# Attention value matmuls placed one unit later, with two tiles for the transposed probabilities, in a cross-attention and expert layer

## The chip, the cores and the metric

The kernel runs on one core of one Trainium2 chip. The metric is the device time of one execution in microseconds. The median of three executions of the kernel before is 782.37 us (781.3 to 784.15).

## The reference, cut to what matters

```
x = x + xattn(layernorm(x), ctx, ctx, pad, sub, Wq, bq, Wk, bk, Wv, bv)
x = x + ffn(layernorm(x), Ws1, bs1, Ws2, bs2, We1, be1, We2, be2, Wr, br)

xattn:  q, k, v = query @ Wq.T + bq, key @ Wk.T + bk, value @ Wv.T + bv     # 16 heads of 16
        att = where(pad or sub is 0, -1e9, q k^T / sqrt(16))
        out = softmax(att) v
ffn:    ys = geglu(x @ Ws1 + bs1) @ Ws2 + bs2                               # shared expert
        logits = (x @ Wr + br) / 1.5 ; top 2 of 12 experts, softmax over the two
        yr = sum over the two of weight * (geglu(x @ We1[e] + be1[e]) @ We2[e] + be2[e])
        return ys + yr
```

x and ctx are (16, 128, 256) in f32: 16 batches of 128 rows. The change is in the attention and in what stands directly before and behind it.

## The kernel before, in words

**Pairs and units.** Attention runs over eight pairs of batches (`pair(p, ...)`, once in the code of each engine). A pair has four units, n = 0 to 3: unit n covers batch n // 2 of the pair and the eight heads of half n % 2. Pair 0 stands alone (`first`), pairs 1 to 4 are a hardware loop of two pairs a turn, pairs 5 and 6 are written out, and so is pair 7 (`last`), which has no projections to make for a next pair.

**What a unit does.** TensorE makes the scores of eight heads in two banks of `ps_s` (`scores`: two mask matmuls, L476, and sixteen small ones, L481). VectorE takes the negated maximum (L1011) and adds it while it copies the scores to SBUF (`softmax_shift`, L1017, tile `prob`); ScalarE takes the exponential in place (`exp`, L775). In the next unit TensorE transposes the probabilities in two halves of four heads (`prob_transposes`, jj = 0 and 1, L493), both into the same bank `ps_t[:, 0]`, and ScalarE copies each half to `probT` (`prob_copy`, L766). The second half can be transposed only when the first has been copied. `values` (L505) then multiplies all eight heads of `probT` by v into `ps_o`. When both halves of a batch are in `ps_o`, ScalarE copies it to `outT` (`out_copy`, L771), TensorE transposes it back (`out_transposes`, L514), and VectorE divides by the row sums (`norm`, L1025 and L1027), adds to x and takes statistics (`residual`, L1035 to L1043). With both batches of a pair added, GpSimd raises the variance to -1/2 (`rstd`, L1286 and L1288) and VectorE writes the second layer norm (`ln2_apply`, L1051).

**The steps of the next pair.** Between a unit's transposes and values stand the steps that prepare pair p + 1: `cT` and `xT` (transposes of context and of normalised x), `k0`, `k1`, `q0`, `q1` (two projections of k and two of q) and `v`; and two for pair p - 1: `r` (transposes of the second layer norm) and `l` (router logits). The table `PLAN` says which steps stand in which unit. Every step takes the next of two PSUM banks (`step_bank`). For `cT` and `xT` ScalarE copies a high part to `aTh` (L743) and VectorE takes the rest to `aTl` (L948); for a k step the two are `k_hi` (L754) and `k_lo` (L958), for a q step `q_cut` (L751) and `q_st` (L955). A step on TensorE waits until the step two before it has left its bank (semaphore `xb_free`), and a pair's first scores wait for every step of the pair before.

**What sets the order.** Each engine runs its own instructions in the order in which its block lists them, and `pair` lists them by hand for each engine: TensorE at L533, ScalarE at L798, VectorE at L1055. An engine that waits holds up everything listed behind. On VectorE, unit 0's `cT` step stands between maximum and shift; `norm(p, 0)` is in unit 2, `norm(p - 1, 1)` in unit 0, and the residuals one unit behind each.

**Before and behind.** Ahead of pair 0 the same seven steps are made once for pair 0 (`PROJ`), with the weights split into high and low parts just ahead of their first use: `weights_hi` on ScalarE (L737), `weights_lo` on VectorE (L940). VectorE makes the masks at the `v` step (L985 to L993); at the `k1` step it waits for the rest of x (semaphore `x_rest_in`) and makes the first layer norm of pair 1 (L903 to L913). SyncE issues the loads. Behind pair 7 the feed-forward part begins (`up`, L583) while the last batch is finished. GpSimd then scatters rows to the experts, and the expert tiles follow. None of these is edited.

Of the kernel before, what the change touches and what calls it, by code (L numbers as in the profile page):

```python
# [17 lines left out]
P = 128  # L18
# [30 lines left out]
def build(nc, x_d, ctx_d, pad_d, sub_d, wq_d, wk_d, wv_d, bq_d, bk_d, bias_d, tab_d, ws1_d, ws2_d, w1_d,  # L49
# [98 lines left out]
    probT = put("probT", [P, 2, 4, P], f32, low)  # L148
# [121 lines left out]
    PLAN = [["cT", "xT", "k0"], ["v", "k1"], ["r", "q0"], ["q1", "l"]]  # L270
# [37 lines left out]
    with block:  # L308
# [3 lines left out]
        def _(sp):  # L312
# [3 lines left out]
            sp.dma_start(wk_raw[:, :, :], wk_d.rearrange("(c p) n -> p c n", p=P)).then_inc(wk_in, 16)  # L316
            sp.dma_start(wv_raw[:, :, :], wv_d.rearrange("(c p) n -> p c n", p=P)).then_inc(wv_in, 16)
            sp.dma_start(wq_raw[:, :, :], wq_d.rearrange("(c p) n -> p c n", p=P)).then_inc(wq_in, 16)
# [93 lines left out]
        def _(pe):  # L412
# [42 lines left out]
            def router(s, q, idx, bank):  # L455

                pe.wait_ge(xb_free, idx - (0 if isinstance(idx, int) and idx == PAIR_STEPS_END + 1 else 1))
# [38 lines left out]
            def values(U, n, par, batch):  # L496
# [4 lines left out]
                for g in range(4):  # L501
                    for jj in range(2):
# [3 lines left out]
                                          probT[:, jj, g, :], start=True, stop=True)  # L506
# [11 lines left out]
            for k, s in enumerate(PROJ):  # L518
                if s == "xT":
                    pe.wait_ge(idents_ready, 1)  # L520
                if s == "k0":
                    pe.wait_ge(w_ready, 1)
                if s == "v":
                    pe.wait_ge(w_ready, 2)
                    pe.wait_ge(bias_ready, 1)
                if s == "q0":
                    pe.wait_ge(w_ready, 3)
                step(s, 0, 0, k, k % 2)
# [4 lines left out]
            def pair(p, par, first, last):  # L533
                for n in range(4):
# [6 lines left out]
                    pn, ppar, pbatch = (n - 1) % 4, par if n else 1 - par, p * 2 + (n - 1) // 2  # L541
# [10 lines left out]
                    if prev:  # L552
                        prob_transposes(p * 4 + n - 1, pn, 0)
                    next_step()
                    if prev:
                        prob_transposes(p * 4 + n - 1, pn, 1)
                    next_step()
                    if prev:
                        values(p * 4 + n - 1, pn, ppar, pbatch)
                    next_step()  # L560
                    if n % 2 == 0 and prev:
# [112 lines left out]
            x_transposes(0, 0, 0)  # L674
            prob_transposes(UNITS - 1, 3, 1)
            values(UNITS - 1, 3, 1, B - 1)
            pe.wait_ge(converted, 1)
            pe.wait_ge(shifted, UNITS)
            up(0, 0, 0, False, SH)
            out_transposes(B - 1)  # L680
            up(0, 0, 1, False, SH)
# [43 lines left out]
        def _(sc):  # L725
# [13 lines left out]
            def step(s, pp, par, idx, bank):  # L739
# [16 lines left out]
                else:  # L756
                    sc.wait_ge(xb_free, idx)
                    act.activation(v_sb[par][:, :, :, 0:HD],
# [3 lines left out]
            def prob_copy(U, jj):  # L762
                sc.wait_ge(pt_ready, 2 * U + jj + 1)
                if not (isinstance(U, int) and U == 0):
                    sc.wait_ge(pv_done, 2 * U + jj - 1)
                act.activation(probT[:, jj, :, :], ps_t[:, 0, :].rearrange("p (g t) -> p g t", g=4),  # L766
# [19 lines left out]
            for k, s in enumerate(PROJ):  # L786
                if k == 1:
                    weights_hi(wkh, wk_raw, wk_in)
                if s == "v":
                    weights_hi(wvh, wv_raw, wv_in)  # L790
                    weights_hi(wqh, wq_raw, wq_in)
# [6 lines left out]
            def pair(p, par, first, last):  # L798
                for n in range(4):
# [13 lines left out]
                    if prev:  # L813
                        prob_copy(U, 0)
                    next_step()
                    if prev:
                        prob_copy(U, 1)
                    if n == 0:
                        next_step()
                    if n % 2 == 0 and prev:  # L820
                        out_copy(p * 2 + (n - 1) // 2)
                    exp(p * 4 + n, n)
# [42 lines left out]
            prob_copy(UNITS - 1, 0)  # L865
            x_hi(0)
            prob_copy(UNITS - 1, 1)
# [22 lines left out]
        def _(ve):  # L890
# [79 lines left out]
            for k, s in enumerate(PROJ):  # L970
# [4 lines left out]
                if s == "v":  # L975
                    weights_lo(wvl, wv_raw, wvh, 1)
                    weights_lo(wql, wq_raw, wqh, 2)
# [77 lines left out]
            def pair(p, par, first, last):  # L1055
                for n in range(4):
# [12 lines left out]
                    if n == 3:  # L1069
# [396 lines left out]
```

## Time and profile before

| | |
|---|---|
| median of three executions | 782.37 us |
| the profiled execution | 781.65 us, span 779.5 us |
| TensorE matmul busy | 640.2 us (82%) |
| VectorE busy | 457.8 us (59%) |
| ScalarE busy | 270.1 us (35%) |
| GpSimd busy | 330.0 us (42%) |
| before the first scores | 0 to 30.3 us |
| attention, pairs 0 to 7 | 30.3 to 256.4 us |
| routing, scatter and expert tiles | 256.4 to 779.5 us |

Busy shares over the whole span mix stages with different limits, so the attention is read pair by pair. In the rows below a time is in microseconds from the span's start. A timeline row gives the start, the duration, the engine, the line, the operation, and what is written from what; where the engine sat idle before it, the idle time and what ended it stand in brackets. SPq is the queue of SyncE. PEclk is the granted TensorE clock as a share of 2.4 GHz, so 0.50 is 1.2 GHz.

### The profile page before, as it was taken

What the parts mean: (1) busy time and instruction counts of PE and PEld (TensorE: products, weight loads), DVE (VectorE), ACT (ScalarE), POOL (GpSimd) and SP (SyncE); (2) the same over time, 40 slices, a digit from 0 to 9 for tenths busy, and PEclk for the clock granted to TensorE, in tenths of its full rate; (3) what the DMA queues carried; (4) which work ended last, traced back from release to release, by engine and by line L of the source; (5) the groups of instructions that cost most, each with busy time, mean ns of one, the idle gap of its engine ahead of it and who ended that gap; (6) DMA issues with size and microseconds to landing.
All of it is one profiled execution on the core that took longest, in us unless ns stands there. A gap on an engine that the chain in (4) does not pass through costs nothing.

```text
span 779.5 us, 16006 instructions
## 1 busy us (share of the span) xinstructions
PE 640.2 (82%) x4977; PEld 590.3 (76%) x4978; DVE 457.8 (59%) x893; ACT 270.1 (35%) x556; POOL 330.0 (42%) x389
## 2 busy tenths in 40 slices
PE   4699899899987776079999999999999999997041
PEld 4577777777865665079999999999999999997041
DVE  4656677676765583056665656656566565663136
ACT  3245555555544311024333333333333333331010
POOL 0610000000000477790847957677878582006710
PEclk9689999999999898579999999999999999999556
DMA  9930101001001143252344435525554241013412
GB/s 305 371 133 15 42 28 40 13 27 42 1 29 41 42 148 109 101 189 61 104 162 150 161 119 191 161 76 193 189 177 153 101 135 40 27 40 99 118 48 81
DMA packets 44289, 83.03 MB, mean 107 GB/s; under 512 B 4832, under 2 KB 32736, under 8 KB 44128
## 3 DMA queue, kind: packets, MB, share of 16 engines
q0 software_dynamic: 11120, 48.24, 18.4%
q1 hardware_dynamic: 32560, 34.04, 13.2%
q10 hardware_dynamic: 576, 0.30, 0.2%
q8 instruction: 21, 0.34, 0.2%
q14 instruction: 12, 0.10, 0.0%
HBM read 60.81 MB, written 19.66 MB: 103 GB/s over the span
## 4 chain that ended last, share of the span: by engine, by line
PE 71%; DVE 8%; another core or an unknown queue 8%; issue 5%; ACT 5%; SPq 1%; DMA 1%; POOL 0%; DVEq 0%; ACTq 0%
PE ps_s L583 27%; PE ps_o L623 15%; PE ps_t L596 5%; PE ps_t L493 4%; PE ps_s L481 4%; PE ps_o L505 4%; PE ps_t L440 3%; ACT probT L766 2%; PE ps_x L440 2%; PE ps_s L476 2%; DVE x_all L1264 2%; PE ps_x L605 1%; DMA br<-in_br 1%; DVE ag L1176 1%
## 5 line engine op out<-in xcount | busy, mean ns | idle before, releaser
L583 PE MATMUL ps_s<-ring,xTh 128*128 (+1 forms) x944 | 203.0, 337 | 4.9 <-issue 4.4
L623 PE MATMUL ps_o<-ring,hTh 128*128 (+1 forms) x644 | 127.3, 297 | 65.6 <-DVE hTl L1188 59.0
L583 PEld LDWEIGHTS ps_s<-ring,xTh 128*128 128x128 f32 x944 | 155.3, 193 | 8.3 <-issue 5.4
L623 PEld LDWEIGHTS ps_o<-ring,hTh 128*128 128x128 f32 x644 | 103.1, 198 | 67.4 <-issue 57.3
L1298 POOL TENSOR_TENSOR ring<-stage,ring 128x512 fp32r<-128x512 f32 x120 | 150.9, 1287 | 2.3
L1176 DVE TENSOR_TENSOR ag<-ps_s,up_bias 128x768 f32<-128x768 f32 (+1 forms) x96 | 88.8, 925 | 67.0 <-PE ps_s L583 45.4
L838 ACT ACTIVATE hTh<-ps_t 128x384 fp32r<-128x384 f32 (+1 forms) x118 | 54.6, 462 | 207.1 <-PE ps_t L596 138.9
L583 PE MATMUL ps_s<-ring,xTl 128*128 (+1 forms) x472 | 115.5, 325 | 2.1 <-issue 2.0
L1286 POOL TENSOR_TENSOR ve<-mv,eps 128x2 f32<-128x2 f32 x16 | 3.1, 197 | 232.4 <-DVE mv L1043 170.9
L623 PE MATMUL ps_o<-ring,hTl 128*128 (+1 forms) x322 | 93.3, 290 | 0.0
L831 ACT ACTIVATE ps_s<-ag 128x384 f32<-128x384 f32 (+1 forms) x118 | 55.1, 467 | 90.7 <-DVE ag L1176 85.4
L583 PEld LDWEIGHTS ps_s<-ring,xTl 128*128 128x128 f32 x472 | 83.8, 192 | 0.6 <-issue 0.6
L1182 DVE TENSOR_TENSOR ag<-ag,ps_s 128x384 f32<-128x384 f32 (+1 forms) x118 | 61.1, 518 | 37.6 <-ACT ps_s L831 31.1
L1188 DVE TENSOR_TENSOR hTl<-ps_t,hTh 128x384 fp32r<-128x384 f32 (+1 forms) x118 | 60.9, 517 | 23.6 <-ACT hTh L838 19.1
L1294 POOL TENSOR_SCALAR ring<-stage 128x512 fp32r<-128x512 f32 x120 | 71.7, 626 | 4.8 <-DVE logits L966 4.0
L596 PE MATMUL ps_t<-const,ag 128*128 128x128 f32 x322 | 57.1, 282 | 8.3 <-issue 7.5
L623 PEld LDWEIGHTS ps_o<-ring,hTl 128*128 128x128 f32 x322 | 63.8, 198 | 0.0
L766 ACT ACTIVATE probT<-ps_t 128x512 f32<-128x512 f32 x64 | 38.2, 596 | 69.5 <-PE ps_t L493 69.5
L1409 POOL DMA_INDIRECT gath<-rows_out,idx_top x32 | 30.8, 961 | 67.1 <-DMA rows_out<-y_row 57.6
L1193 DVE TENSOR_TENSOR xTl<-ps_x,xTh 128x256 fp32r<-128x256 f32 x59 | 25.0, 424 | 50.9 <-ACT xTh L845 44.5
L596 PEld LDWEIGHTS ps_t<-const,ag 128*128 128x128 f32 x322 | 38.5, 143 | 15.0 <-issue 10.4
L1011 DVE TENSOR_REDUCE nmax<-ps_s 128x8 f32<-128x1024 f32 x32 | 39.0, 1220 | 16.6 <-PE ps_s L481 16.5
(194 smaller groups left out, 1018.6 us busy)
## 6 DMA issues: line engine op xcount, KB each, us to landing
stage<-in_w POOLq DMA_DIRECT2D x12, 1536.0 KB, 6.7
stage<-in_w POOLq DMA_DIRECT2D x12, 768.0 KB, 5.4
up_bias<-in_bias POOLq DMA_DIRECT2D x12, 768.0 KB, 4.8
rows_in<-y_row SPq DMA_DIRECT2D x1, 5504.0 KB, 22.3
xrow<-rows_in SPq DMA_DIRECT2D x43, 128.0 KB
rows_out<-y_row SPq DMA_DIRECT2D x43, 128.0 KB, 1.7
cbuf<-in_ctx SPq DMA_DIRECT2D x8, 256.0 KB, 3.2
xn_all<-xn2p SPq DMA_DIRECT2D x8, 256.0 KB, 2.4
```

The costliest lines, as they stand in the source:

```text
L583: last = pe_.matmul(out, x[:, c, :], weights(place, a, half_w), start=n == 0, stop=n == 5)
L596: last = pe_.transpose(ps_t[:, u, c * P:(c + 1) * P], ag[u][:, 0, c * P:(c + 1) * P], ident)
L623: pe_.matmul(ps_o[:, 0:D], h[u][:, c, :], weights(place, a, D), start=n == 0, stop=False)
L766: act.activation(probT[:, jj, :, :], ps_t[:, 0, :].rearrange("p (g t) -> p g t", g=4), ACT.Identity).then_inc(pt_copied, 1)
L831: act.activation(ps_s[:, 2 * u + 1, 0:half_w], ag[u][:, 1, 0:half_w], ACT.Gelu).then_inc(gelu_done[u], 1)
L838: act.activation(hTh[u][:, 0:nch, :], ps_t[:, u, 0:nch * P].rearrange("p (c n) -> p c n", c=nch), ACT.Identity).then_inc(ht_hi[u], 1)
L1011: vec.tensor_reduce(nmax[:, :, :], src, AX.X, ALU.max, negate=True).then_inc(maxed, 1)
L1176: vec.tensor_tensor(ag[u][:, :, 0:half_w], ps_s[:, 2 * u:2 * u + 2, 0:half_w], bias, ALU.add)\
L1182: vec.tensor_tensor(ag[u][:, 0, 0:half_w], ag[u][:, 0, 0:half_w], ps_s[:, 2 * u + 1, 0:half_w], ALU.mult)\
L1188: vec.tensor_tensor(hTl[u][:, 0:nch, :], ps_t[:, u, 0:nch * P].rearrange("p (c n) -> p c n", c=nch), hTh[u][:, 0:nch, :].bitcast(f32), ALU ...
L1294: last = pool.tensor_scalar(hi_ap[:, c:c + PIECE], src[:, c:c + PIECE], 1.0, 0.0, ALU.mult, ALU.add)
L1298: last = pool.tensor_tensor(lo_ap[:, c:c + PIECE], src[:, c:c + PIECE], hi_ap[:, c:c + PIECE].bitcast(f32), ALU.subtract)
```

## The change

`probT` becomes two tiles, taken by turns of the unit. On TensorE `values` of unit n - 2 stands between the two halves of the transposes of unit n - 1, and `out_transposes` stands at the end of units 1 and 3 in place of 0 and 2. `PLAN` moves `q0` to unit 1, `v` alone to unit 2, and `r`, `q1`, `l` to unit 3. ScalarE takes the exponential and the `out_copy` ahead of the second `prob_copy`. VectorE has `norm`, `residual` and `ln2_apply` one unit later. Ahead of pair 0 the v weights come after the q weights, in the loads as well.

```diff
@@ -145,7 +145,10 @@
 ...
     prob = [put(f"prob{i}", [P, 2, 4, P], f32, low) for i in range(2)]
-    probT = put("probT", [P, 2, 4, P], f32, low)
+    probT = [put("probT0", [P, 2, 4, P], f32, low)]
+    spare = [ring_at + 2 * SLOT_W * 4 + 2 * (W1S + W2S) * 4]
+    probT.append(put("probT1", [P, 2, 4, P], f32, spare))
+    assert spare[0] <= ring_at + 3 * SLOT_W * 4
     assert low[0] <= ring_at + 2 * SLOT_W * 4, low[0] - ring_at - 2 * SLOT_W * 4
@@ -267,7 +270,7 @@
-    PLAN = [["cT", "xT", "k0"], ["v", "k1"], ["r", "q0"], ["q1", "l"]]
+    PLAN = [["cT", "xT", "k0"], ["k1", "q0"], ["v"], ["r", "q1", "l"]]
     PROJ = [s for unit in PLAN for s in unit if s not in "rl"]
@@ -314,8 +317,8 @@
 ...
             sp.dma_start(wk_raw[:, :, :], wk_d.rearrange("(c p) n -> p c n", p=P)).then_inc(wk_in, 16)
+            sp.dma_start(wq_raw[:, :, :], wq_d.rearrange("(c p) n -> p c n", p=P)).then_inc(wq_in, 16)
             sp.dma_start(wv_raw[:, :, :], wv_d.rearrange("(c p) n -> p c n", p=P)).then_inc(wv_in, 16)
-            sp.dma_start(wq_raw[:, :, :], wq_d.rearrange("(c p) n -> p c n", p=P)).then_inc(wq_in, 16)
             sp.dma_start(sub_b[:, :], sub_d).then_inc(mask_in, 16)
@@ -454,7 +457,7 @@
 ...
-                pe.wait_ge(xb_free, idx - (0 if isinstance(idx, int) and idx == PAIR_STEPS_END + 1 else 1))
+                pe.wait_ge(xb_free, idx - (0 if isinstance(idx, int) and idx in (PAIR_STEPS_END - 1, PAIR_STEPS_END + 1) else 1))
                 ps = step_bank[bank]
@@ -503,7 +506,7 @@
 ...
                         last = pe_.matmul(ps_o[32 * j:32 * j + VW, g * P:(g + 1) * P], v_sb[par][:, b, h, :],
-                                          probT[:, jj, g, :], start=True, stop=True)
+                                          probT[n % 2][:, jj, g, :], start=True, stop=True)
                         if g == 3:
@@ -520,11 +523,11 @@
 ...
                     pe.wait_ge(w_ready, 1)
+                if s == "q0":
+                    pe.wait_ge(w_ready, 2)
                 if s == "v":
-                    pe.wait_ge(w_ready, 2)
+                    pe.wait_ge(w_ready, 3)
                     pe.wait_ge(bias_ready, 1)
-                if s == "q0":
-                    pe.wait_ge(w_ready, 3)
                 step(s, 0, 0, k, k % 2)
@@ -538,7 +541,8 @@
 ...
                     prev = not (first and n == 0)
-                    pn, ppar, pbatch = (n - 1) % 4, par if n else 1 - par, p * 2 + (n - 1) // 2
+                    behind = not (first and n < 2)
+                    pn, ppar, pbatch = (n - 2) % 4, par if n >= 2 else 1 - par, p * 2 + (n - 2) // 2
@@ -550,15 +554,15 @@
 ...
                     if prev:
-                        prob_transposes(p * 4 + n - 1, pn, 0)
+                        prob_transposes(p * 4 + n - 1, (n - 1) % 4, 0)
                     next_step()
+                    if behind:
+                        values(p * 4 + n - 2, pn, ppar, pbatch)
                     if prev:
-                        prob_transposes(p * 4 + n - 1, pn, 1)
+                        prob_transposes(p * 4 + n - 1, (n - 1) % 4, 1)
                     next_step()
-                    if prev:
-                        values(p * 4 + n - 1, pn, ppar, pbatch)
                     next_step()
-                    if n % 2 == 0 and prev:
+                    if n % 2 == 1 and behind:
                         out_transposes(pbatch)
@@ -672,13 +676,14 @@
 ...
             x_transposes(0, 0, 0)
+            values(UNITS - 2, 2, 1, B - 1)
             prob_transposes(UNITS - 1, 3, 1)
-            values(UNITS - 1, 3, 1, B - 1)
             pe.wait_ge(converted, 1)
 ...
             up(0, 0, 0, False, SH)
+            values(UNITS - 1, 3, 1, B - 1)
+            up(0, 0, 1, False, SH)
             out_transposes(B - 1)
-            up(0, 0, 1, False, SH)
             router("r", PAIRS - 1, PAIR_STEPS_END, 0)
@@ -755,15 +760,17 @@
 ...
                     sc.wait_ge(xb_free, idx)
+                    if not (isinstance(pp, int) and pp < 2):
+                        sc.wait_ge(pv_done, pp * 8 - 8)
                     act.activation(v_sb[par][:, :, :, 0:HD],
 ...
-            def prob_copy(U, jj):
+            def prob_copy(U, n, jj):
                 sc.wait_ge(pt_ready, 2 * U + jj + 1)
-                if not (isinstance(U, int) and U == 0):
-                    sc.wait_ge(pv_done, 2 * U + jj - 1)
-                act.activation(probT[:, jj, :, :], ps_t[:, 0, :].rearrange("p (g t) -> p g t", g=4),
+                if not (isinstance(U, int) and U < 2):
+                    sc.wait_ge(pv_done, 2 * U - 2)
+                act.activation(probT[n % 2][:, jj, :, :], ps_t[:, 0, :].rearrange("p (g t) -> p g t", g=4),
                                ACT.Identity).then_inc(pt_copied, 1)
@@ -786,9 +793,10 @@
 ...
                     weights_hi(wkh, wk_raw, wk_in)
+                if s == "q0":
+                    weights_hi(wqh, wq_raw, wq_in)
                 if s == "v":
                     weights_hi(wvh, wv_raw, wv_in)
-                    weights_hi(wqh, wq_raw, wq_in)
                 if s == "k0":
@@ -811,15 +819,13 @@
 ...
                     if prev:
-                        prob_copy(U, 0)
+                        prob_copy(U, (n - 1) % 4, 0)
                     next_step()
+                    exp(p * 4 + n, n)
+                    if n % 2 == 1 and not (first and n < 2):
+                        out_copy(p * 2 + (n - 2) // 2)
                     if prev:
-                        prob_copy(U, 1)
-                    if n == 0:
-                        next_step()
-                    if n % 2 == 0 and prev:
-                        out_copy(p * 2 + (n - 1) // 2)
-                    exp(p * 4 + n, n)
+                        prob_copy(U, (n - 1) % 4, 1)
                     next_step()
@@ -862,9 +868,9 @@
 ...
-            prob_copy(UNITS - 1, 0)
+            prob_copy(UNITS - 1, 3, 0)
             x_hi(0)
-            prob_copy(UNITS - 1, 1)
+            prob_copy(UNITS - 1, 3, 1)
             out_copy(B - 1)
@@ -973,8 +979,9 @@
 ...
                 if s == "v":
-                    weights_lo(wvl, wv_raw, wvh, 1)
-                    weights_lo(wql, wq_raw, wqh, 2)
+                    weights_lo(wvl, wv_raw, wvh, 2)
+                if s == "q0":
+                    weights_lo(wql, wq_raw, wqh, 1)
                     vec.tensor_scalar(bqc[:, :], bqs[:, :], const[:, C_LOQ:C_LOQ + 1], None, ALU.mult)\
@@ -1066,20 +1073,20 @@
 ...
                     softmax_shift(p * 4 + n, n, next_step if n == 0 and todo else None)
-                    if n == 3:
-                        residual(p, 0)
-                    if n == 1 and not first:
+                    further = not last and not (isinstance(p, int) and p + 2 >= PAIRS)
+                    if n == 0 and not first:
+                        residual(p - 1, 0)
+                    if n == 2 and not first:
                         residual(p - 1, 1)
-                    further = not last and not (isinstance(p, int) and p + 2 >= PAIRS)
-                    if n == 1 and not first:
-                        ln2_apply(p - 1)
                     if n == 2 and further:
                         ln1_stats(p + 2)
-                    if n == 2:
-                        norm(p, 0)
                     while todo:
                         next_step()
-                    if n == 0 and not first:
+                    if n == 2 and not first:
+                        ln2_apply(p - 1)
+                    if n == 3:
+                        norm(p, 0)
+                    if n == 1 and not first:
                         norm(p - 1, 1)
@@ -1220,6 +1227,7 @@
 ...
+            residual(PAIRS - 1, 0)
             x_lo(0)
```

**TensorE, unit 0 of a pair in the loop, behind its scores.** `ps_t` and `ps_x` are PSUM banks, the number behind `prob` and `probT` tells the tile. Before:

```order
L493 MATMUL ps_t<-const,prob_119 128x128 x4
L425 REGISTER_ALU
L431 ISA
L417 MATMUL ps_x<-const,cbuf 128x128 x4
L491 REGISTER_ALU
L493 MATMUL ps_t<-const,prob_119 128x128 x4
L417 MATMUL ps_t<-const,xn_121 128x128 x4
L498 REGISTER_ALU
L505 MATMUL ps_o<-probT,v_sb_116 32x128 x8
```

Of the change:

```order
L496 MATMUL ps_t<-const,prob_119 128x128 x4
L428 REGISTER_ALU
L434 ISA
L420 MATMUL ps_x<-const,cbuf 128x128 x4
L501 ISA
L503 REGISTER_ALU
L508 MATMUL ps_o<-probT_120,v_sb_116 32x128 x8
L494 REGISTER_ALU
L496 MATMUL ps_t<-const,prob_119 128x128 x4
L420 MATMUL ps_t<-const,xn_122 128x128 x4
```

The values now read the other `probT` and stand between the two halves, where before they came behind both.

**ScalarE, unit 3 of a pair in the loop.** Before, the whole unit:

```order
L766 ACTIVATE probT<-ps_t 128x512
L741 REGISTER_ALU
L751 ACTIVATE q_cut<-ps_t,bqc,const 128x256 x2
L763 ISA
L766 ACTIVATE probT<-ps_t 128x512
L774 REGISTER_ALU
L775 ACTIVATE prob_119<-prob_119 128x1024
```

Of the change, from the router's copy to the unit's end:

```order
L790 ACTIVATE xn2T<-ps_x 128x512
L781 REGISTER_ALU
L782 ACTIVATE prob_119<-prob_119 128x1024
L777 ISA
L778 ACTIVATE outT<-ps_o 128x512
L770 REGISTER_ALU
L773 ACTIVATE probT_120<-ps_t 128x512
L746 REGISTER_ALU
L756 ACTIVATE q_cut<-ps_t,bqc,const 128x256 x2
```

The last q projection's `q_cut` was ahead of the unit's exponential; it is now behind the exponential and two copies.

**VectorE, ahead of pair 0, from the k1 step on.** `wql` and `wvl` are the low parts of the q and v weights, `xn` the first layer norm of pair 1. Of the change:

```order
L964 SCALAR_TENSOR_TENSOR k_lo_114<-ps_t,bks,k_hi_112 128x256 x2
L1004 MEMSET v_sb_116 128x32x15
L1005 MEMSET v_sb_116 128x32
L1004 MEMSET v_sb_117 128x32x15
L1005 MEMSET v_sb_117 128x32
L909 BN_STATS bn_67<-x_all 128x6 x2
L911 MEMSET tick 128x1
L913 BN_AGGR mv_68<-bn_67 128x2 x2
L919 TENSOR_SCALAR xn_122<-x_all,mv_68,rs_70 128x256 x2
L946 TENSOR_TENSOR wql<-wq_raw,wqh 128x1024
L985 TENSOR_SCALAR bqc<-bqs,const 128x4
L961 SCALAR_TENSOR_TENSOR q_st_110<-ps_x,bqs,q_cut 128x256 x2
```

Before, `wvl` and `wql` stood ahead of the masks, of the k1 step's `k_lo` and of the wait for the rest of x; now `wql` stands behind that wait, and `wvl` behind the first `q_st`.

## Rows read from the trace of the kernel before

**Rows 1.** Stretches of pairs 0, 3 and 7: PE, PEld, DVE, ACT, POOL busy us (instructions), PEclk, DMA.

```profile
30.30:62.30 32.00, 28.51 (x218) 23.44 (x218) 17.34 (x30) 13.14 (x22) 10.86 (x12) 0.75 0.52 183
...
118.10:145.98 27.88, 25.58 (x259) 21.58 (x259) 19.42 (x43) 15.09 (x26) 1.77 (x4) 1.00 0.09 28
...
228.80:256.40 27.60, 20.27 (x215) 15.05 (x215) 14.10 (x25) 11.79 (x18) 0.88 (x2) 1.00 0.10 30
```

**Rows 2.** Timeline of TensorE in pair 3.

```profile
138.87 0.66 PE L514 MATMUL ps_o<-const,outT 128*128 128x128 f32 x4 [0.72 <-ACT outT L771]
```

**Rows 3.** Timeline of ScalarE in pair 3.

```profile
129.81 0.59 ACT L766 ACTIVATE probT<-ps_t 128x512 f32<-128x512 f32 x1
130.29 1.05 ACT L775 ACTIVATE prob<-prob 128x1024 f32<-128x1024 f32 x1
131.24 0.84 ACT L754 ACTIVATE k_hi<-ps_x,bks 128x256 fp32r<-128x256 f32 x2
...
139.66 1.01 ACT L751 ACTIVATE q_cut<-ps_x,bqc,const 128x256 fp32r<-128x256 f32 x2
```

**Rows 4.** Timeline of VectorE in pair 3.

```profile
122.16 1.22 DVE L1017 TENSOR_TENSOR prob<-ps_s,nmax 128x1024 f32<-128x1024 f32 x1
...
126.04 0.88 DVE L958 SCALAR_TENSOR_TENSOR k_lo<-ps_x,bks,k_hi 128x256 fp32r<-128x256 f32 x2 [2.06 <-ACT k_hi L754]
126.83 0.25 DVE L1025 RECIPROCAL rden<-ps_o 128x16 f32<-128x16 f32 x1
...
127.46 1.22 DVE L1011 TENSOR_REDUCE nmax<-ps_s 128x8 f32<-128x1024 f32 x1
128.80 1.23 DVE L1017 TENSOR_TENSOR prob<-ps_s,nmax 128x1024 f32<-128x1024 f32 x1
129.94 0.41 DVE L1035 TENSOR_TENSOR x_all<-x_all,att 128x256 f32 x1
...
132.39 0.74 DVE L1051 TENSOR_SCALAR xn2p<-x_all,mv,rs 128x256 f32 x2 [1.29 <-POOL rs L1288]
133.04 0.87 DVE L958 SCALAR_TENSOR_TENSOR k_lo<-ps_x,bks,k_hi 128x256 fp32r<-128x256 f32 x2
...
144.78 0.86 DVE L955 SCALAR_TENSOR_TENSOR q_st<-ps_t,bqs,q_cut 128x256 fp32r<-128x256 f32 x2
145.55 0.17 DVE L966 TENSOR_TENSOR logits<-ps_x,br 128x24 f32 x1
```

**Rows 5.** Timeline of SyncE's queue at the start.

```profile
4.35 0.45 SPq L321 DMA_DIRECT2D x_all<-in_x  x1
```

**Rows 6.** DMA issues at the start: tile, queue, count, KB, us from issue to landing.

```profile
x_all<-in_x SPq DMA_DIRECT2D x1, 1792.0 KB, 13.7
```

**Rows 7.** Timeline of VectorE at the start.

```profile
15.12 1.22 DVE L940 TENSOR_TENSOR wql<-wq_raw,wqh 128x1024 fp32r<-128x1024 f32 x1
...
27.30 1.32 DVE L913 TENSOR_SCALAR xn<-x_all,mv,rs 128x256 f32<-128x256 f32 x2 [1.08 <-POOL rs L1288]
```

**Rows 8.** Timeline of TensorE at the start.

```profile
15.26 0.79 PE L448 MATMUL ps_t<-wvh,aTh 128*128 128x256 f32 x2 [2.59 <-DVE wvl L940]
...
18.41 0.63 PE L440 MATMUL ps_x<-aTh,wkh 128*128 128x256 f32 x2
```

**Rows 9.** TensorE by stretch: length, busy us (instructions), granted clock, DMA share, GB/s.

```profile
49.70:53.00 3.30, 1.42 (x19) 1.00 0.00 0
53.00:60.30 7.30, 7.30 (x41) 0.53 0.00 0
26.00:39.40 13.40, 8.51 (x40) 0.50 1.08 381
```

**Rows 10.** Timeline of TensorE behind pair 7.

```profile
252.63 0.66 PE L493 MATMUL ps_t<-const,prob 128*128 128x128 f32 x4
...
257.92 0.60 PE L514 MATMUL ps_o<-const,outT 128*128 128x128 f32 x4
```

**Rows 11.** Timeline of VectorE behind pair 7.

```profile
258.79 0.25 DVE L1025 RECIPROCAL rden<-ps_o 128x16 f32<-128x16 f32 x1
```

## The prediction

> **What bounds the kernel now.** I read the engines by stretch first, one stretch for each pair [rows 1]. In pair 3 TensorE is busy for 25.58 of 27.88 us, VectorE for 19.42 and ScalarE for 15.09. TensorE is the fullest engine but not a full one: 2.30 us of each pair are gaps. The timeline of TensorE names them: it waits for ScalarE to copy the first half of the transposed probabilities before it can make the second, for the second copy before the values, and once for `outT`, 0.72 us [rows 2]. Those are the gaps at which the edit aims, 2.3 us in each of six steady pairs. Next I read the timelines of ScalarE and VectorE [rows 3, 4], since the edit reorders both. They run in order, so the question is not how busy they are but how long the row of handovers is that leads from one pair's first scores to the next pair's. The start and the end of the attention have rows of their own [rows 5 to 8, 10, 11], and the clock has [rows 9].
>
> **The steady pair, laid out in its new order.** Times are from the pair's first score matmul, 118.10 in pair 3. A handover between engines costs 0.03 to 0.05 us (`q_cut` ends at 140.67, `q_st` could start at 140.70), and one engine's next instruction starts a fixed step after the last: 0.48 us after a copy, 0.95 after an exponential, 1.01 for `q_cut` [rows 3].
> - Unit 0. Up to the shift nothing moves: it starts at 4.06 and ends at 5.28 [rows 4]. ScalarE now takes the exponential at 5.32, the second copy at 6.27, the copy of `xT` at 6.76, `k_hi` from 7.25 to 8.09. VectorE: `k_lo` from 8.12, and its step to the next instruction is 0.79.
> - Unit 1. Maximum at 8.91, shift 1.34 later at 10.25, ending at 11.47. Exponential 11.51, `outT` copy 12.46, second copy 12.95, `q_cut` of `q0` from 13.44 to 14.45. `q_st` at 14.48, 0.80 later `norm` at 15.28, which takes 0.63 (126.83 to 127.46).
> - Unit 2. Maximum 15.91, shift 17.25, residual 1.14 later at 18.39. From residual to `ln2_apply` are 2.45 us (129.94 to 132.39, GpSimd's power between), so 20.84, and 0.65 more until VectorE is free.
> - Unit 3. Maximum 21.49, shift 22.83 to 24.05. Exponential 24.09, `outT` copy 25.04, second copy 25.53, `q_cut` of `q1` 26.02 to 27.03. `q_st` 27.06, logits 0.77 later (144.78 to 145.55), and 0.43 after those the next pair's scores, which wait for every step: **28.26 us**.
>
> TensorE's own work in this order, about 25 us, is never last in that row. It waits at three places: under 0.2 us for `aTl` ahead of `k1`, about 0.8 us ahead of `r`, since `ln2_apply` now ends at 21.6 while the scores of unit 3 end at 20.4, and about 1.7 us at the pair's end. So the three waits for copies go, and a wait of the same sum comes in their place, because `q_cut` of the last projection stood ahead of the exponential and now stands behind it and two copies. 28.26 against 27.88 is +0.38 a pair, for pairs 1 to 6 **+2.3 us**. Each of some twenty handovers may be off by 0.03, so between -0.2 and +0.9 a pair, -1 to +5 us.
>
> [...]
>
> **The start.** The split of the q weights moves behind the wait for the rest of x. That load is issued at 4.35 [rows 5] and lands 13.7 later, at 18.05 [rows 6]. Then, on VectorE: statistics 1.0, GpSimd's power 1.2, the first piece of `xn` and its step about 0.7 (it took 1.32 for both pieces, with GpSimd at work beside it [rows 7]), so 20.9; `wql` 1.22 [rows 7], 22.1. The seven steps' last four are now a serial row: `q0` at 1.2 GHz (v's fourteen matmuls took 3.15 from 15.26 to 18.41 [rows 8], twelve of them some 2.9 with the first load) to 25.0; `q_cut` and `q_st` 2.0, 27.0; `wvl` 0.65, 27.6; `v` 3.15, 30.8; `q1` between 1.7 and 2.9, say 2.2, 33.0; `q_cut`, `q_st` and handovers 2.1, so first scores at 35.1 where they were at 30.3: **+4.8 us**, between +3.5 and +5.5. The masks, 4.96 us of VectorE, end at 33 and stay hidden beside `v` and `q1`. The swapped loads of wq and wv cost nothing: both have landed by then. The shared expert's weights are loaded later, since SyncE waits for the third split, and are converted at about 35 to 46 instead of 27 to 38; their first reader starts at 256, so 200 us cover that.
>
> **Pair 0** took 32.0 us [rows 1], and TensorE was at 1.2 GHz (0.50) for the first 9 us of it and for 7.3 us from 53.0 [rows 9]. The second stretch comes behind 3.3 us in which TensorE was busy for 1.42, waiting for the second copy and for `outT`. Neither wait is left in the new order: laid out as above, with the first scores, transposes and `k0` at 1.2 GHz again, the pair takes 27.2 us: **-4.8 us**. Of that 3.3 to 3.7 are the cold stretch, half of 7.3, and the rest its waits. If the clock is up from the first scores on, the pair takes 24.4 (-7.6); if it falls again, some 30.5 (-1.5).
>
> **Pair 7 and behind it.** Pair 7 has no projections, and TensorE is busy for 20.27 of 27.60 us [rows 1]. Laid out the same way with its own steps the last transposes of probabilities start at 21.4 instead of 23.8 after the pair's start (252.63 [rows 10]). Then `values`, first half of `up`, last `values`, second half of `up`, and `outT`'s transposes at 27.6 where they were at 257.92, 29.1. `norm` on VectorE waited 0.87 behind them for a bias [rows 10, 11]; it now starts at 28.5 instead of 30.0. **-1.5 us**, between 0 and -3. What follows, router, choice of experts and GpSimd's scatter, has no other cover and shifts by the same.
>
> **The sum**: +4.8 - 4.8 + 2.3 - 1.5 = **+0.8 us** on the profiled execution's 781.65 (span 779.5 and 2.15 around it). The median of the runs is 782.37, 0.7 above, so the median of the change should be 783.2. A measurement of this kernel tells about 0.5%, 3.9 us, from no change; the forecast is no change.
>
> **Rival A, slower: the clock falls at a pair's end.** The new wait is one piece of some 1.7 us, and ahead of it stand the router's narrow matmuls and four transposes. In pair 0 before, a stretch with 1.88 of 3.3 us idle was followed by 7.3 us at half clock [rows 9]; in pair 7, as idle on the whole but in pieces of 0.8 or less, the clock stayed at 1.00 [rows 1]. It decides once the clock falls at two pair ends. A fall costs up to half of 7.3 us, and since VectorE and ScalarE wait behind the cold scores, transposes and `k0`, about 3.3 us arrive; in two or three of the seven pair ends that is 7 to 10 us: 791 us. For it: the likeness to 49.7 to 53.0. Against: the gap may be 1.2 as well as 1.7. Chance 0.33.
>
> The Trainium skill says that the throttled state is the default and activity releases it (TensorE: Matmul & The Clock Gate, Part 1). The trace agrees, with 0.50 from 26.0 to 39.4 although TensorE was busy for 8.51 of these 13.4 us [rows 9]; it does not say which gap is enough here.
>
> **Rival B, faster: the gaps close.** If VectorE and ScalarE are less bound to each other than I lay them out, TensorE's work of about 25.6 us sets the pair: -2.3 in six pairs, -13.8 in place of +2.3, which gives 767. For it: VectorE is 70% and ScalarE 54% busy in a pair. Against: the row of handovers above, each link of which is in the listed order. Chance 0.1. [...]
>
> **Rival C, faster by the clock alone.** Pair 0 at full clock from its first scores, and pair 7 at its better bound: +4.8 - 7.6 + 1.3 - 3 = -4.5, 778. For it: `v` and `q1` stand closer to the first scores. Against: two idle microseconds between them, and the clock took until 39.3 before. Chance 0.15.
>
> **The numbers.** The forecast, +0.8 with -3 to +4, has 0.42. The range that holds the time 8 times in 10 reaches into rivals A and C: 774 to 794. Faster by over 0.5%: B, most of C and a little of the forecast, 0.22. Slower by over 0.5%: A and a little of the forecast, 0.36. Within: 0.42.
>
> **What would show it.** Right: first scores near 35; pairs 1 to 4 at 28.0 to 28.6; in them no wait of TensorE for a `probT` copy, a wait for `xn2p` of 0.8 ahead of `r`, one of 1.2 to 2 for VectorE's logits ahead of a pair's scores; pair 0 near 27. Wrong: pairs near 25.6 (B), or PEclk under 1.00 in pairs 1 to 6 (A); first scores at or before 32 would break the start's term.

## The result, and the profile after

| | before | after |
|---|---|---|
| median | 783.26 us (4 runs, 781.3 to 787.16) | 794.07 us (4 runs, 791.45 to 795.52) |
| profiled execution | 781.65 us, span 779.5 | 791.45 us, span 789.3 |
| first scores of pair 0 | 30.34 us | 34.55 us |
| pair 0 | 32.0 us | 28.01 us |
| pairs 1 to 6 | 166.4 us | 176.8 us |
| pair 7, to the last `outT` transposes | 29.1 us | 32.7 us |
| from there to the scatter's start | 32.3 us | 30.9 us |

After / before is 1.0157, with a 95% interval of 1.0106 to 1.0208: 1.6% slower. The forecast was no change, and 794.07 lies just past the range's upper end.

The table adds up to +4.2 - 4.0 + 10.3 + 3.6 - 1.4 = +12.7 us at the scatter's start; the end is 9.8 us later, since some 3 us come back behind the first gather (issued at 705.14 before and at 717.79 after, still 12.65 us apart), in work that the change doesn't touch. Why they come back was not looked for. Two terms, the start and pair 0, cancel as forecast. The loss lies in pairs 1 to 7.

The page of the changed kernel has the clock by slices of 19.7 us. Attention is slices 2 to 14:

```profile
PE 656.0 (83%) x4977; PEld 601.4 (76%) x4978; DVE 457.8 (58%) x893; ACT 270.8 (34%) x556; POOL 330.9 (42%) x389
...
PEclk9579998898997979659999999999999999999666
```

TensorE is 15.8 us busier than before, with the same matmuls. By stretch, one for each of pairs 1 to 6, and one for pair 7 up to shortly before the last `outT` transposes (columns as in [rows 1]):

```profile
62.50:90.70 28.20, 25.81 (x261) 21.52 (x258) 19.81 (x43) 15.11 (x26) 1.90 (x4) 1.00 0.08 29
90.70:119.90 29.20, 26.91 (x258) 22.51 (x259) 19.72 (x42) 15.31 (x26) 1.90 (x4) 0.94 0.09 28
119.90:150.40 30.50, 28.46 (x258) 23.62 (x258) 19.59 (x42) 15.30 (x26) 1.91 (x4) 0.89 0.08 26
150.40:180.70 30.30, 28.46 (x258) 23.81 (x258) 19.42 (x41) 15.36 (x26) 1.90 (x4) 0.89 0.08 26
180.70:210.80 30.10, 28.52 (x258) 24.06 (x258) 19.60 (x42) 15.32 (x26) 1.80 (x4) 0.89 0.08 27
210.80:239.30 28.50, 26.91 (x258) 22.66 (x258) 18.58 (x37) 15.22 (x26) 0.89 (x2) 0.94 0.06 20
239.30:265.00 25.70, 22.92 (x185) 16.99 (x185) 13.73 (x24) 9.86 (x15) 0.89 (x2) 0.73 0.10 31
```

Pair 1, the only steady pair in which the clock stayed at 1.00, took 28.18 us from scores to scores (forecast 28.26). From there on the granted clock drops, and pairs 3 to 5 take some 2 us more, about what TensorE is busier (28.46 against 25.81). VectorE and ScalarE are as busy as in pair 1. Where in the pair the clock drops, from TensorE alone (length, busy us, granted clock, DMA share, GB/s):

```profile
90.70:92.70 2.00, 1.96 (x22) 0.99 0.00 0
92.70:97.00 4.30, 4.30 (x33) 0.61 0.23 65
97.00:119.90 22.90, 20.65 (x208) 1.00 0.07 24
119.90:127.00 7.10, 7.10 (x46) 0.52 0.12 37
150.40:158.00 7.60, 7.57 (x51) 0.55 0.12 35
180.70:189.00 8.30, 8.25 (x55) 0.59 0.12 34
```

Pairs start at 90.74, 119.90, 150.43 and 180.75. The granted clock goes to its lower level, 1.2 GHz (0.50), between 0 and 2 us behind a pair's start, and comes back some 3.4 us (pairs 2 and 6) or 6.8 us (pairs 3 to 5) later; a mean such as 0.59 over 8.3 us is part low and part full clock (8.3 x 0.41 / 0.50 = 6.8). Ahead of each of these starts stands the new wait, here at the end of pair 1, from the timelines of TensorE, ScalarE and VectorE:

```profile
86.54 1.06 ACT L782 ACTIVATE prob<-prob 128x1024 f32<-128x1024 f32 x1 [1.11 <-DVE prob L1024]
87.50 0.58 ACT L778 ACTIVATE outT<-ps_o 128x512 f32<-128x512 f32 x1
87.98 0.59 ACT L773 ACTIVATE probT<-ps_t 128x512 f32<-128x512 f32 x1
88.46 1.02 ACT L756 ACTIVATE q_cut<-ps_t,bqc,const 128x256 fp32r<-128x256 f32 x2
89.52 0.88 DVE L961 SCALAR_TENSOR_TENSOR q_st<-ps_t,bqs,q_cut 128x256 fp32r<-128x256 f32 x2 [3.01 <-ACT q_cut L756]
90.31 0.17 DVE L972 TENSOR_TENSOR logits<-ps_x,br 128x24 f32 x1
90.74 0.60 PE L479 MATMUL ps_s<-mask_b,ident_b 128*128 x2 [1.65 <-DVE logits L972]
```

Read from the bottom: the next pair's scores (`ps_s`) waited 1.65 us for the logits, these stand behind `q_st`, that waited for `q_cut`, and `q_cut` stood behind the exponential and two copies. The waits of TensorE over pairs 1 to 6 (in total, how often, the longest), before and after:

```profile
PE ps_o L514 <- ACT outT L771: 4.4, 6, 0.7
PE ps_t L493 <- ACT probT L766: 4.0, 12, 0.3
PE ps_o L505 <- ACT probT L766: 3.7, 12, 0.4
PE ps_s L476 <- DVE logits L966: 0.9, 3, 0.3
```

```profile
PE ps_s L479 <- DVE logits L972: 9.1, 6, 1.6
PE ps_t L420 <- DVE xn2p L1058: 1.3, 3, 0.6
PE ps_x L420 <- DVE xn2p L1058: 1.1, 3, 0.5
PE ps_o L517 <- ACT outT L778: 0.3, 1, 0.3
```

The sum is about the same, 13.0 and 11.8 us. Before, it came in 33 pieces of 0.7 us or less; after, 9.1 us come in six pieces of 1.36 to 1.65 us, at the ends of pairs 1 to 6. The first five stand ahead of the falls in pairs 2 to 6, the sixth ahead of the first fall in pair 7; the second fall there, at about 253, comes behind a wait of 1.98 us for `outT` (ahead of 251.91).

### The profile page after: what moved, and what is told of

The parts are those of the page before. It is cut to its first block, busy times and chain, and to the rows that moved or that the text cites. A ratio compares the mean times of both kernels' runs of the same rounds, so it can differ in the third digit from the quotient of the medians.

```text
span 789.3 us, 16008 instructions
## 1 busy us (share of the span) xinstructions
PE 656.0 (83%) x4977; PEld 601.4 (76%) x4978; DVE 457.8 (58%) x893; ACT 270.8 (34%) x556; POOL 330.9 (42%) x389
## 3 DMA queue, kind: packets, MB, share of 16 engines
HBM read 60.81 MB, written 19.66 MB: 102 GB/s over the span
## 4 chain that ended last, share of the span: by engine, by line
PE 65%; DVE 12%; another core or an unknown queue 8%; issue 7%; ACT 4%; DMA 2%; POOL 1%; SPq 0%; DVEq 0%; ACTq 0%; POOLq 0%
PE ps_s L587 26%; PE ps_o L627 14%; PE ps_t L600 5%; PE ps_s L484 4%; PE ps_t L496 3%; PE ps_o L508 3%; DVE nmax L1018 2%; PE ps_t L443 2%; PE ps_x L443 2%; DVE prob L1024 2%; DVE x_all L1272 2%; DMA x_all<-in_x 2%; PE ps_s L479 2%; PE ps_x L609 1%
## 5 line engine op out<-in xcount | busy, mean ns | idle before, releaser
L587 PEld LDWEIGHTS ps_s<-ring,xTh 128*128 128x128 f32 x944 | 153.7, 191 | 11.7 <-issue 5.5
L1417 POOL DMA_INDIRECT gath<-rows_out,idx_top x32 | 30.9, 965 | 67.2 <-DMA rows_out<-y_row 57.7
```

The lines of the kernel that those rows point to most:

```text
L587: last = pe_.matmul(out, x[:, c, :], weights(place, a, half_w), start=n == 0, stop=n == 5)
```

## The experiments

**Theory 1** (the prediction's rival A): the wait in one piece at the pair's end lets the clock fall. **Theory 2**: the pairs are longer because VectorE and ScalarE hand over more slowly; the clock is a side effect. The start is a third, separate matter.

The kernel before takes 731 to 735 us in the experiments' sessions, in place of 783; they ran on two chips, and whether the result came from one of these is not on record. There is one trace of the kernel before, from the first session. The changed kernel's steady pairs agree between the sessions wherever its clock does the same (with the old start, below, to 0.04 us in each of pairs 1 to 6), and most of the difference lies behind the scatter. So ratios to the kernel before are compared, and within the attention the traces' own times. The ratios' base moves too, by some 4 us from one session to the next. In the diffs "+" is added to the kernel named.

### The gap filled, nothing else moved

To the changed kernel, in TensorE's `pair`, ahead of a pair's first scores; the real mask matmuls then overwrite the bank:

```diff
+                        if not first:
+                            pe.wait_ge(shifted, p * 4 - 1)
+                            for _ in range(7):
+                                pe_.matmul(ps_s[:, 0, :].rearrange("p (g t) -> p g t", g=4), ident_b[:, :],
+                                           mask_b[:, 0:1, :].broadcast_to([P, 4, P]), start=True, stop=True)
```

> The change, with seven extra mask matmuls of 512 columns (some 1.6 us) on TensorE ahead of its wait for a pair's first scores, written into a bank that the scores then overwrite; nothing else moves. Theory 1 (the clock): the new wait of 1.4 to 1.7 us at a pair's end lets the clock fall, and pairs 2 to 6 pay for it. With the gap filled PEclk is 1.00 in pairs 1 to 6, each pair takes 28.2 us (27.9 in pairs 5 and 6), and the median falls by about 8 us, to 786. Theory 2 (the handovers between ScalarE and VectorE set the pair, and the clock only follows): the pairs keep their 29.2 to 30.5 us and the median stays at 794.

Ratio 0.9996 (0.9958 to 1.0033), 730.57 us. Two of its pairs (TensorE alone):

```profile
115.90:143.90 28.00, 27.21 (x267) 1.00 0.08 28
143.90:172.00 28.10, 27.33 (x268) 1.00 0.09 28
```

TensorE does 1.67 us more work a pair and the kernel is faster: the clock stays at 1.00 and the pair takes 28.1 instead of 30.5. This gives back all of the loss (1.0207 in these sessions, below), and it is theory 1's result. Against the changed kernel there the last `outT` transposes come 10.8 us earlier (256.70 against 267.46), and the medians differ by 11.8. What remains in pairs 2 to 4 against before's 27.9 is 0.2 to 0.4 us a pair, the longer row of handovers.

**Three of these matmuls in place of seven** (`range(3)`):

> The change with three added mask matmuls instead of seven in front of each following unit's first scores, which leave about 1.0 us of TensorE's 1.65 us gap at the pair's end. If the clock falls because of the whole gap, a gap of about 1 us should bring back most of it: pairs 3 to 6 between 28.0 and 28.8 us, ratio to the kernel before 0.999 to 1.008. If only a filled gap helps, pairs 3 to 6 stay at 29.5 to 30.5 us and the ratio near 1.018. If the clock has nothing to do with the gap, the ratio is that of the change, 1.016 to 1.021.

Ratio 0.9948 (0.9897 to 1.0000), 726.96 us. The pairs run as with seven, 28.06 us at a clock of 1.00, although TensorE still waits at the pair's end:

```profile
143.60:171.70 28.10, 26.46 (x264) 1.00 0.09 28
...
PE ps_s L479 <- DVE logits L977: 4.9, 6, 0.9
```

The line on the wait covers pairs 1 to 6. Waits of 0.7 to 0.9 us at their ends kept the clock; in the change, those of 1.36 to 1.65 us did not. The gap need not be closed, only made shorter. Whether the shorter wait does it or the 0.81 us of added work beside it, this run can't tell apart; the next one shortens the wait without adding work. The ratio came out below the 0.999 to 1.008 that was expected. The pairs are those of the run with seven to 0.01 us, so what is better than 0.9996 lies outside them, or in the base.

### The order of ScalarE put back

In the changed kernel, ScalarE's `pair`, directly behind `exp(p * 4 + n, n)`:

```diff
+                    if n == 3:
+                        next_step()
```

> The change, with ScalarE taking the q_cut of q1 directly behind the exponential of unit 3, ahead of the outT copy and the second probability copy. By the rows of the changed kernel q_cut comes 0.97 us earlier, so the gap at a pair's end shrinks from 1.65 to about 0.7. Theory 1 (the clock): 0.97 us a pair for the order and the whole cold time besides: PEclk 1.00, pairs of 27.3 us, median near 780. Theory 2 (handovers alone): 0.97 us in six pairs, median near 788, with cold stretches left.

Ratio 0.9898 (0.9830 to 0.9965), 724.09 us: faster than the kernel before, by a little more than its spread. Pairs 2 to 6 take 27.83, 27.55, 27.35, 26.99 and 26.99 us, the clock is 1.00, and no wait for logits is left (waits from 62 to 220 us):

```profile
PE ps_o L517 <- ACT outT L778: 5.5, 11, 0.8
PE ps_t L420 <- DVE xn2p L1060: 1.4, 3, 0.7
PE ps_x L420 <- DVE xn2p L1060: 1.3, 3, 0.5
```

So one instruction group's place on ScalarE made the loss, not the second tile or the later values. Not all of the gain over the kernel before is the pairs': pairs 1 to 6 take 164.3 us in place of 166.45, and pair 0 took 24.9 in place of 32.0, which changes from run to run (below).

### That one reordering, alone in the kernel before

ScalarE's `pair` of the kernel before; everything else stays (one `probT`, the old `PLAN`, the old start):

```diff
-                    next_step()
+                    if n != 3:
+                        next_step()
```

> The kernel before, with one thing of the change alone: in unit 3 ScalarE takes q_cut of q1 behind the exponential instead of ahead of it. By the rows of before the first scores of the next pair come 1.3 us later, with a gap of about 1.6 us ahead of them. Theory 1 (the clock): PEclk falls in most pairs and they take 29 to 30.5 us, the median rises by 12 to 18 us over 783. Theory 2 (handovers alone): 1.3 us in six pairs, +8 us, and PEclk stays at 1.00.

Ratio 1.0402 (1.0325 to 1.0479), 758.96 us, more than the change lost, and twice what was expected (28 us over the kernel before, where 12 to 18 were). Pairs 2, 4 and 5 (TensorE alone), and the row at pair 3's start:

```profile
92.80:124.30 31.50, 28.20 (x259) 0.90 0.09 26
...
154.30:183.40 29.10, 25.53 (x259) 1.00 0.08 27
183.40:214.70 31.30, 28.50 (x258) 0.89 0.08 26
```

```profile
124.29 0.60 PE L476 MATMUL ps_s<-mask_b,ident_b 128*128 x2 [2.07 <-DVE logits L967]
```

Pair 4 kept its clock, and so parts the two prices: 29.04 from scores to scores against 27.68 before is the longer row of handovers, +1.4 us; pairs 2 and 5, at 31.4, pay the fallen clock as well, up to 2.4 us more. Waits of 1.8 to 2.1 us stood at every pair's end, and behind the 2.07 us ahead of pair 4 the clock did not fall.

The part that nobody expected is pair 7. Its length to the last `outT` transposes went from 29.1 to 37.6 us, a third of the 25.7 us that the kernel has lost by then, though the edit reorders nothing in its first three units; ahead of it stands a wait of 1.78 us. From TensorE alone, before and here:

```profile
228.80:257.90 29.10, 21.77 (x226) 1.00 0.09 28
```

```profile
246.05:266.05 20.00, 16.35 (x96) 0.50 0.02 6
246.05:283.60 37.55, 30.42 (x226) 0.69 0.07 21
```

The clock fell just ahead of the pair and stayed down for 20 us, where it came back within 7 in the changed kernel's falls. The waits in these 20 us are of 0.8 us or less, as before the change, where the clock was up and stayed up with them.

### The start put back

The changed kernel with before's steps, loads and splits ahead of pair 0 (`PROJ` written out in its old order, wv loaded and split ahead of wq):

```diff
-    PROJ = [s for unit in PLAN for s in unit if s not in "rl"]
+    PROJ = ["cT", "xT", "k0", "v", "k1", "q0", "q1"]
```

> The change, with the steps ahead of pair 0 and the loads and splits of the q and v weights in the order of before; the pairs are untouched. First scores at 30.3 instead of 34.6. If the start is a cost of its own, the time falls by its 4.2 us, to about 790. Rival: pair 0 was 4 us shorter in the changed kernel only because TensorE's clock was in another phase after the later start; then pair 0 goes back to 31 to 32 us and the time stays at 793 to 794.

Ratio 1.0111 (1.0044 to 1.0177), 739.11 us. First scores at 30.34 us as before, and pairs 2 to 6 at 29.16, 30.51, 30.36, 30.09 and 28.54 as in the change: the start has nothing to do with the clock in the steady pairs. Pair 0 took 24.93 us and not the 31 to 32 of the expectation's rival, the same as with the late start in the next run, so its shortness does not hang on the late start.

**The change itself in these sessions**, for a ratio under the same conditions:

> The changed kernel itself, beside the other three on one chip. Both theories: pairs 2 to 5 at 29 to 30.5 us with PEclk under 1.00, ratio to the kernel before 1.010 to 1.020. If the 1.0157 had been chance of a chip, the ratio would be 1.00.

Ratio 1.0207 (1.0159 to 1.0254), 742.37 us. Three of its pairs show the clock falling one pair later than in the first trace, and then in each (in the run with the old start, on the same chip as this one, it fell from pair 2 on):

```profile
88.70:117.00 28.30, 25.72 (x258) 1.00 0.08 29
117.00:146.00 29.00, 26.93 (x259) 0.94 0.08 27
146.00:176.20 30.20, 28.37 (x258) 0.89 0.08 26
```

The old start is worth 1.0207 - 1.0111 = 0.0096, or 7 us at 731, with intervals that overlap, while the medians differ by 3.3 us and the traces by 4.2 us at pair 7's start (236.32 against 232.10). The ratios' two bases lie some 4 us apart, which is the difference.

### Both repairs together, and a stronger one

The ScalarE order and the old start:

> The change with both corrections: q_cut of q1 directly behind the exponential of unit 3, and the start of before. If the start is a cost of its own, first scores at 30.3 and 4 to 6 us under the kernel with the order alone (724.1 in its session, ratio 0.990), so ratio 0.983. If the gain of pair 0 hangs on the late start, ratio 0.990 again.

Ratio 0.9922 (0.9899 to 0.9944), 721.70 us, against 0.9898 for the order alone. The expected 0.983 did not come. In the traces pair 1 starts 4.6 us earlier (56.75 against 61.35): 5.8 at the first scores, of which pair 0, at 26.09 us in place of 24.9, gives back 1.2. The medians differ by 2.4 us. The ratio shows nothing of it, because the kernel before, run beside each, was itself 4 us faster here (721.70 / 0.9922 = 727.4 against 724.09 / 0.9898 = 731.6).

Then the last q projection goes forward on both engines, on TensorE to directly behind the router's transposes and on ScalarE ahead of the exponential, where it stood before the change; with the old start:

```diff
@@ TensorE, pair, behind the first next_step()
+                    if n == 3 and not last:
+                        next_step()
@@ ScalarE, pair, ahead of exp(p * 4 + n, n)
+                    if n == 3 and not last:
+                        next_step()
```

> The change with the start of before, and in unit 3 TensorE makes q1 directly behind r, ahead of the values, and ScalarE takes its q_cut ahead of the exponential. If the place of q_cut in ScalarE's order sets the pair's end, first scores no longer wait for the logits' chain, TensorE sets the pair, which takes 26.3 to 26.8 us, ratio 0.975 to 0.980. Rival: the shift and exponential of unit 3 are late anyway (ln2_apply stands ahead of them on VectorE) and the pair stays at 27.3 or more, ratio 0.985.

Ratio **0.9855 (0.9827 to 0.9883)**, 716.95 us: faster than both kernels, though not the 0.975 to 0.980 that was expected. The pairs came as expected: pair 3 takes 26.70 us, 1.2 less than before, and TensorE is busy for 25.75 of them:

```profile
109.75:136.45 26.70, 25.75 (x258) 21.67 (x259) 19.67 (x41) 15.11 (x26) 1.91 (x4) 1.00 0.09 29
```

```profile
133.45 1.02 ACT L758 ACTIVATE q_cut<-ps_t,bqc,const 128x256 fp32r<-128x256 f32 x2 [0.82 <-PE ps_t L443]
134.37 1.05 ACT L784 ACTIVATE prob<-prob 128x1024 f32<-128x1024 f32 x1
```

`q_cut` now fills 0.92 us of ScalarE's wait for the shifted scores, and the exponential follows it at once.

The same with the change's own, later start:

> The same early q1, with the changed kernel's own start. Against the run with the start of before it prices the start alone while the clock stays up in the pairs: 4.2 us more if the start is a cost of its own, nothing if the clock in pair 0 gives it back.

Ratio 0.9874 (0.9817 to 0.9931), 720.54 us. Pairs are the same to 0.01 us; pair 1 starts at 60.81 us instead of 55.91. So the late start costs 4.9 us in the trace and 3.6 in the medians, once nothing else differs.

### A miss: another gap filled

In the fastest kernel the clock falls once more, in pair 7. Its longest wait there is 1.34 us for `outT` in unit 1, 8 us ahead of the fall. Six of the mask matmuls were put ahead of it:

```diff
+                    if last and n == 1:
+                        pe.wait_ge(shifted, p * 4 + 1)
+                        for _ in range(6):
+                            pe_.matmul(ps_s[:, 0, :].rearrange("p (g t) -> p g t", g=4), ident_b[:, :],
+                                       mask_b[:, 0:1, :].broadcast_to([P, 4, P]), start=True, stop=True)
```

> The kernel with q_cut ahead of the exponential and the start of before (0.9855 of before) with six mask matmuls added ahead of the outT transposes of unit 1 in pair 7, where TensorE waits 1.3 us and the clock fell. If the gap is what lets the clock fall, it stays up through pair 7 and the last outT transposes come 1 to 3 us earlier: ratio 0.981 to 0.984. If not, the ratio is 0.9855 again, or worse by the added matmuls' 1.3 us.

Ratio 0.9845 (0.9765 to 0.9926), 718.92 us, an interval that holds every outcome that was expected; the traces decide. The matmuls stand in the gap (1.46 us from 226.42), and the clock falls all the same, 15.5 to 23.5 us behind the pair's start in both kernels; the unfilled one first:

```profile
231.30:235.30 4.00, 2.99 (x24) 0.76 0.30 105
235.30:239.30 4.00, 3.75 (x32) 0.82 0.33 96
```

```profile
234.00:238.00 4.00, 3.01 (x24) 0.75 0.34 119
238.00:242.00 4.00, 3.75 (x33) 0.83 0.27 82
```

The last `outT` transposes start 28.6 us behind the pair's start in both. The wait I filled was not the one that counts here: in the first of the two stretches TensorE is idle for 1.0 of 4 us, in pieces of 0.7 or less. So here the clock fell without a long wait close ahead of it. Which of the pieces lets the clock go, or whether the transfers of that stretch have a part in it, is open; it wasn't tried.

## Why the prediction was wrong

- **The row of handovers** was right: 28.26 us a pair laid out, 28.18 measured with the clock up. Over pairs 1 to 6 it is worth +0.9 us (167.35 with the gap filled against 166.45 before) where +2.3 was forecast: pairs 1 to 4 lose 0.2 to 0.4 us each, and pairs 5 and 6, written out, lose nothing (27.50 us against 27.57 and 27.56). The waits came where they were placed: 1.65 us for the logits (forecast 1.7), 0.6 or less for `xn2p` (forecast 0.8), and none left for a `probT` copy. That rival B fell has the same cause: the copies' waits went, and the row of handovers, not TensorE's work, set the pair.
- **The clock at the pair's end is the step that failed.** The sum had no term for it; it stood as rival A, with a chance of 0.33 and two or three falls of 3.3 us. It fell in each of pairs 2 to 6, for 0.9 to 2.6 us each against the same pairs with the gap filled, 176.8 - 167.4 = +9.4 us in all, and twice in pair 7. The size of one fall was overestimated, their number underestimated. What was weighed wrongly is the evidence. Both rows that rival A names speak for it: pair 0, where a long idle piece came ahead of 7.3 us at half clock [rows 9], and pair 7, as idle in the sum but never for more than 0.8 us in a piece, at 1.00 [rows 1]. The edit was about to make a piece of 1.7 us in each pair, and the only reason given against was that it might be 1.2. Still the sum priced it at nothing. The filled gap showed it: the same order with seven matmuls more a pair is 2% faster, and with three as well.
- **The start**: +4.8 forecast, +4.2 measured; first scores at 34.55 instead of 35.1, because `wql` started at 20.49 (forecast 20.9) and the projections behind it were a little quicker:

```profile
20.49 1.22 DVE L946 TENSOR_TENSOR wql<-wq_raw,wqh 128x1024 fp32r<-128x1024 f32 x1
```

- **Pair 0**: -4.8 forecast, -4.0 measured (28.01 us). In eight of the nine later runs of kernels with the changed order it took 24.9 to 26.1 us, and once 28.4, all between the forecast's bounds of 24.4 and 30.5. It changes from run to run (24.93 and 28.01 us for one kernel), so that -4.8 and -4.0 lie so close together is in part luck.
- **Pair 7**: -1.5 forecast, +3.6 measured. The layout had the clock at 1.00; it was 0.73 over the stretch. With the gap filled, the last transposes come 28.1 us behind the pair's first real scores (228.60 to 256.70), 1.0 earlier than before: the sign of the layout was right, the clock turned it.

By its terms the sum of +0.8 became +4.2 - 4.0 + 0.9 + 9.4 + 3.6 = +14.1 us at the last `outT` transposes: start, pair 0, handovers, clock in pairs 2 to 6, pair 7.

With the order of the change the second tile came with a slower kernel, with `q_cut` ahead of the exponential with a faster one, 0.9855. The tile alone does not decide; the order of ScalarE around it does.

## What to carry to other kernels

When an edit gathers many short waits of TensorE into one, the sum says little: 33 waits of up to 0.7 us left the clock at 1.00, and five of 1.4 to 1.65 us cost 9.4 us more than themselves. Lay out the row of handovers from one turn's start to the next (it was right to 0.1 us in pair 1, and 0.8 too long for pairs 5 and 6), look for the longest single wait in it, and give that wait a price in clock, or fill it with a few matmuls that nobody reads. And when a second buffer frees an engine's order, look at what the reordering pushed behind: here one step of ScalarE, moved from behind two copies to directly behind the exponential, turned a loss of 2.1% into a gain of 1.0%, and ahead of the exponential, with its matmuls, into one of 1.3 to 1.5%.

## What the runs showed of the hardware that was not expected

- The clock falls behind a single wait of 1.4 to 1.65 us although TensorE is busy for 25.8 of 28.2 us. It does not fall each time: 1.65 us at the end of pair 1 was followed by 4.3 us at 0.61 in the first trace and in the run with the old start, and by no fall in the later run of the changed kernel. With 0.7 to 0.9 us it did not fall in any of the steady pairs. Nor does length alone decide: a wait of 1.34 us in pair 7 of the run with seven matmuls (ahead of 238.04) was followed by no fall, and in the last experiment the clock fell behind waits of 0.6 and 0.7 us.
- Once down, the clock can stay down with waits that it survives when up: 20 us at 0.50 in pair 7 of the kernel before with the one reordering (246.05 to 266.05), with TensorE busy for 16.35 of them.
- A fall costs less than half of its length: 7.1 us at 0.52 in pair 3 made TensorE 2.65 us busier and the pair 2.35 us longer, so not all of the work in it takes twice as long.
- The granted clock of a trace's first microseconds can be wrong. The fourteen matmuls of `v` ahead of pair 0 took 3.15 us in both traces (the second window takes in the first of the next step), which show 1.00 for them before the change and 0.50 after it; the prediction's 1.2 GHz for them came from their duration and was right:

```profile
15.26:18.41 3.15, 3.15 (x14) 1.00 1.03 255
```

```profile
27.37:30.52 3.15, 3.15 (x15) 0.50 0.62 191
```

- The kernel before takes 783 us in one session and 731 in others, and the changed kernel 794 and 742. In the first session the clock by slices ends in 666 after the change and in 556 before it, where the later traces end in 985 or 995. The stretch from the scatter to the first gather takes 415 us there in both kernels (303.00 to 717.79 after the change) and 392 in the run with seven matmuls. The cause was not looked for.
